# A new order of the last cross attention, and the last head pair's sums of exponentials from TensorE alone

## The reference, cut to what matters

```python
x = layernorm(x + L1_attn(x))       # L1_attn returns x + softmax(q k^T / 8) v w_o
x = layernorm(x + L1_xattn(ctx, x)) # the change ends here
x = layernorm(x + L1_ffn(x))        # 4 experts, two chosen for each token

def L1_xattn(x, latents, mask, ...):       # x: 154 context rows, latents: 512 rows
    xn, ln = layernorm(x, ...), layernorm(latents, ...)
    q  = ln @ Wq.T
    kv = concat([xn @ Wkv.T, ln @ Wlkv.T], axis=1)      # 154 + 512 keys
    k, v = kv[..., :128], kv[..., 128:]                 # 2 heads of 64
    qn, kn = rmsnorm(q, qn_g) * 64 ** -0.5, rmsnorm(k, kn_g)
    attn = softmax(where(mask, qn kn^T, -max))
    return (attn @ v) @ Wo.T + bo
```

## Time and profile before

| | us |
|---|---|
| median of 3 runs | 696.09 (694.47 to 698.51) |
| profiled execution | 697.45 |
| its span, first to last instruction | 695.7 |

### The profile page before, as it was taken

One profiled execution on the slowest core, in us unless ns is written; L12 is line 12 of the kernel. 1 busy time (PEld: TensorE's weight loads), 2 busy tenths in 40 slices (PEclk: granted clock), 3 DMA queues, 4 the chain that ended last, 5 costly groups with the idle time before them and its releaser, 6 DMA issues.

```text
span 695.7 us, 8771 instructions
## 1 busy us (share of the span) xinstructions
PE 617.9 (89%) x3161; PEld 307.6 (44%) x3162; DVE 451.1 (65%) x1172; ACT 287.3 (41%) x548; POOL 246.7 (35%) x178
## 2 busy tenths in 40 slices
PE   8766769998997899999999979997878999999996
PEld 4322457976752322222224422333522446565655
DVE  6999998457679457666765597687626673333234
ACT  7979966032403564444443344341141342212120
POOL 2897443233501554554464444572150100000001
PEclk9957979999998999999999999998997999999999
DMA  8200032030000000000000000001400000000000
GB/s 316 93 0 0 2 121 124 1 122 1 1 1 0 0 1 0 1 0 1 2 0 1 1 0 1 0 1 63 195 0 1 1 1 1 0 1 0 1 1 31
DMA packets 3681, 18.92 MB, mean 27 GB/s; under 512 B 917, under 2 KB 2198, under 8 KB 3126
## 3 DMA queue, kind: packets, MB, share of 16 engines
q1 hardware_dynamic: 3638, 18.36, 6.9%
HBM read 17.84 MB, written 0.52 MB: 26 GB/s over the span
## 4 chain that ended last, share of the span: by engine, by line
PE 62%; DVE 20%; ACT 9%; issue 5%; POOL 4%; POOLq 0%; DVEq 0%; ACTq 0%
PE PS L2339 10%; PE PS L1617 8%; PE PS L2353 6%; DVE SB L1846 6%; PE PS L1562 4%; PE PS L1601 4%; PE PS L1585 3%; PE PS L1687 2%; PE PS L1631 2%; PE PS L2063 2%; DVE SB L199 2%; PE PS L2074 1%; DVE SB L1868 1%; ACT SB L468 1%; POOL SB L238 1%
## 5 line engine op out<-in xcount | busy, mean ns | idle before, releaser
L1832 POOL TENSOR_TENSOR SB<-SB 128x1024 f32<-128x1024 f32 x32 | 75.3, 2353 | 115.3 <-ACT SB L1785 115.3
L1846 DVE TENSOR_REDUCE SB<-PS 128x2 f32<-128x1024 f32 x64 | 78.4, 1225 | 56.7 <-PE PS L1585 56.7
L1785 ACT ACTIVATE SB<-PS 128x1024 f32<-128x1024 f32 x64 | 65.5, 1023 | 101.3 <-PE PS L1604 101.2
L2339 PE MATMUL PS<-SB 128*128 128x512 f32 x176 | 83.1, 609 | 0.2 <-DVE SB L2416 0.2
L1617 PE MATMUL PS<-SB 128*64 128x512 f32 x256 | 69.9, 628 | 1.4 <-DVE SB L1871 1.4
L1601 PE MATMUL PS<-SB 64*128 64x512 f32 x256 | 68.9, 616 | 1.1 <-ACT SB L1789 1.1
L238 POOL TENSOR_TENSOR SB<-SB 128x4 f32<-128x4 f32 x18 | 19.4, 1078 | 133.0 <-DVE SB L204 132.9
L2391 ACT ACTIVATE SB<-PS 128x512 f32<-128x512 f32 (+1 forms) x48 | 28.5, 596 | 90.2 <-PE PS L2339 87.3
L2416 DVE TENSOR_TENSOR SB<-SB,PS 128x512 f32<-128x512 f32 (+1 forms) x48 | 32.6, 686 | 48.1 <-PE PS L2339 43.7
L2353 PEld LDWEIGHTS PS<-SB 128*128 128x128 f32 (+1 forms) x384 | 49.4, 190 | 18.5 <-issue 10.0
L1868 DVE RECIPROCAL SB<-PS 128x512 f32<-128x512 f32 x16 | 53.7, 3355 | 3.9 <-PE PS L1631 3.9
(11 more groups left out here) (401 smaller groups left out, 1132.8 us busy)
## 6 DMA issues: line engine op xcount, KB each, us to landing
SB<-exp SPq DMA_DIRECT2D x1, 4352.0 KB, 14.0
SB<-moe SPq DMA_DIRECT2D x1, 4096.0 KB, 12.3
SB<-dft SPq DMA_DIRECT2D x1, 2304.0 KB, 12.1
SB<-att SPq DMA_DIRECT2D x1, 2048.0 KB, 8.1
SB<-mix SPq DMA_DIRECT2D x1, 768.5 KB, 4.5
SB<-mix SPq DMA_DIRECT2D x1, 640.0 KB, 5.6
SB<-ssm SPq DMA_DIRECT2D x1, 602.0 KB, 6.7
SB<-lat SPq DMA_DIRECT2D x1, 585.0 KB
```

The costliest lines, as they stand in the source:

```text
L1785: act.activation(expd[i % 2][:, 1024 * u:1024 * u + 1024], bank(2 * (u % 2), 2), ACT.Exp).then_inc(sem("d_exp"), 1)
L1832: pool.tensor_tensor(half_sums[half], e[:, 0:1024], e[:, 1024:], ALU.add).then_inc(sem("d_half_sum"), 1)
L1846: dve.tensor_reduce(shift[i % 2][:, qt:qt + DK + 1:DK], two_heads(bank(4, 2)), AX_X, ALU.max, negate=True)\
L2339: pe.matmul(bank(2 * (i % 3) + side), exp_w["e_w13"][:, c:c + 128], xsT[:, 512 * n:512 * n + 512], start=True, stop=True).then_inc(sem(("t ...
```

## The change

It does the following.
- Pair 16's sums: GpSimd's three adds for it go; `sums(15)` multiplies the ones by the four chunks of exponentials, eight matmuls. Its `weigh` writes bank 0 instead of 6 and no longer waits for pair 15's product; the output projection goes to bank 6 instead of 0.
- The two turns of batch 0's rows move behind the context's, out of the loop; the four `weigh` and the sums of pair 16 stand together ahead of all `e_maxima(0, ...)`, which are spread over the output projection, the last one behind it.
- GpSimd makes the powers k = 0 to 2 at the same place as before.
- VectorE takes maximum(0, 0), then pair 16's reciprocal and product, maxima 1 and 2, the residual add and its statistics, maximum 3, and `shift_in(0)` behind the second norm's statistics.
- Cross attention, batch 0: the turn of the normalized rows stands ahead of `score(0, 0)`, the projections of batch 1's rows behind it, their turns behind `score(0, 3)` and `weigh(0, 2)`, batch 1's maxima among the last scores and weighs, `shifts(1)` ahead of `sums(0)`. ScalarE and VectorE follow; VectorE's `late_sum` stands between batch 1's maxima 1 and 2.

```diff
@@ -1564,6 +1564,9 @@
+    def heads_bank(i):
+        return bank(6 if i < NP_ - 1 else 0)
+
@@ -1610,25 +1613,32 @@
-                if i >= 1:
+                if 1 <= i < NP_ - 1:
...
-                ins = pe.matmul(bank(6)[head(h), :], v, expd[i % 2][:, 1024 * kt + 512 * h:1024 * kt + 512 * h + 512],
+                ins = pe.matmul(heads_bank(i)[head(h), :], v, expd[i % 2][:, 1024 * kt + 512 * h:1024 * kt + 512 * h + 512],
...
         def sums(i):
-            pe.wait_ge(sem("d_key_sum"), i + 1)
+            if i < NP_ - 1:
+                pe.wait_ge(sem("d_key_sum"), i + 1)
+                parts = [key_sum]
+            else:
+                pe.wait_ge(sem("d_exp"), 4 * NP_)
+                parts = [expd[i % 2][:, 1024 * kt:1024 * kt + 1024] for kt in range(4)]
...
-            for h in range(2):
-                ins = pe.matmul(bank(7)[DK * h:DK * h + DK, :], ones[:, 0:DK], two_heads(key_sum)[:, h, :], start=True, stop=True)
+            for k, part in enumerate(parts):
+                for h in range(2):
+                    ins = pe.matmul(bank(7)[DK * h:DK * h + DK, :], ones[:, 0:DK], two_heads(part)[:, h, :],
+                                    start=(k == 0), stop=(k == len(parts) - 1))
@@ -1676,7 +1686,7 @@
-                    pe.matmul(bank(0)[:, 128 * t:128 * t + 128], headed[:, at:at + 128],
+                    pe.matmul(bank(6)[:, 128 * t:128 * t + 128], headed[:, at:at + 128],
@@ -1733,9 +1743,6 @@
-                if i == NP_ - 1 and u == 3:
-                    e_turn_tiles(pe, 0)
-                    e_turn_tiles(pe, 1)
@@ -1745,23 +1752,25 @@
-        weigh(last, 0)
-        weigh(last, 1)
+        e_turn_tiles(pe, 0)
+        e_turn_tiles(pe, 1)
+        for kt in range(4):
+            weigh(last, kt)
+        sums(last)
         e_maxima(pe, 0, 0)
-        weigh(last, 2)
-        weigh(last, 3)
+        pe.wait_ge(sem("d_headed"), last)
+        pe.matmul(bank(6), zeros_low, mask_16[0:1, 0:512], start=True, stop=False)
+        attended_part((0,))
         e_maxima(pe, 0, 1)
-        sums(last)
-        pe.matmul(bank(0), zeros_low, mask_16[0:1, 0:512], start=True, stop=False)
-        attended_part((0, 1))
+        attended_part((1, 2))
         e_maxima(pe, 0, 2)
-        attended_part((2, 3))
-        e_maxima(pe, 0, 3)
+        attended_part((3,))
...
-            ins = pe.matmul(bank(0)[:, 128 * t:128 * t + 128], headed[:, 512 * last + 128 * t:512 * last + 128 * t + 128],
+            ins = pe.matmul(bank(6)[:, 128 * t:128 * t + 128], headed[:, 512 * last + 128 * t:512 * last + 128 * t + 128],
...
+        e_maxima(pe, 0, 3)
@@ -1820,10 +1829,7 @@
     def d_pool(pool):
-        for i in range(NP_):
-            if i == NP_ - 1:
-                for k in range(3):
-                    e_pool_row_norms(pool, k)
+        for i in range(NP_ - 1):
@@ -1835,6 +1841,8 @@
+        for k in range(3):
+            e_pool_row_norms(pool, k)
@@ -1868,7 +1876,7 @@
-            dve.tensor_tensor(headed[:, 512 * i:512 * i + 512], bank(6), unit, ALU.mult).then_inc(sem("d_headed"), 1)
+            dve.tensor_tensor(headed[:, 512 * i:512 * i + 512], heads_bank(i), unit, ALU.mult).then_inc(sem("d_headed"), 1)
@@ -2018,7 +2026,7 @@
     def rough_at(b, qt):
-        return 512 * (1 if b == 0 else 0 if qt % 2 else 5)
+        return 512 * (1 if b == 0 else 0 if qt == 2 else 5)
@@ -2030,10 +2038,10 @@
-        if n == 5:
+        if n == 6:
             pe.wait_ge(sem("d_exp"), 4 * NP_ + KT)
-        if b == 0 and qt or b == 1 and qt >= 2:
-            pe.wait_ge(sem("d_max"), 4 * NP_ + n - b)
+        elif qt:
+            pe.wait_ge(sem("d_max"), 4 * NP_ + n - n // 7)
@@ -2049,14 +2057,12 @@
         def shifts(b):
             pe.wait_ge(sem("d_max"), 4 * NP_ + 4 * b + 4)
-            pe.transpose(bank(6)[:, 0:128], e_shift[b], ident).then_inc(sem("d_shifts"), 1)
+            pe.transpose(bank((7, 6)[b])[:, 0:128], e_shift[b], ident).then_inc(sem("d_shifts"), 1)
         def score(b, u):
...
-            if n == 0:
-                pe.wait_ge(sem("e_attended"), 3)
@@ -2078,7 +2084,7 @@
         def sums(b):
             if b == 0:
-                pe.wait_ge(sem("d_max"), 4 * NP_ + 7)
+                pe.wait_ge(sem("d_max"), 4 * NP_ + 8)
@@ -2101,25 +2107,31 @@
+        turn_half(pe, tiled(xn), "e_normed", 1, 1, 5)
         score(0, 0)
-        for u in range(KT):
-            if u + 1 < KT:
-                score(0, u + 1)
-            if u == 2:
-                turn_half(pe, tiled(xn), "e_normed", 1, 1, 5)
-            weigh(0, u)
-            if u == 3:
-                e_project(pe, 4)
-                e_project(pe, 5)
-            if u == 4:
-                e_project(pe, 6)
-                e_project(pe, 7)
+        e_project(pe, 4)
+        e_project(pe, 5)
+        score(0, 1)
+        e_project(pe, 6)
+        e_project(pe, 7)
+        weigh(0, 0)
+        score(0, 2)
+        weigh(0, 1)
+        score(0, 3)
         e_turn_tiles(pe, 2)
+        weigh(0, 2)
         e_turn_tiles(pe, 3)
-        for qt in range(4):
-            e_maxima(pe, 1, qt)
+        score(0, 4)
+        weigh(0, 3)
+        e_maxima(pe, 1, 0)
+        score(0, 5)
+        e_maxima(pe, 1, 1)
+        weigh(0, 4)
+        weigh(0, 5)
+        e_maxima(pe, 1, 2)
+        e_maxima(pe, 1, 3)
+        shifts(1)
         sums(0)
-        shifts(1)
@@ -2147,26 +2159,25 @@
         def turned_rows(b):
-            act.wait_ge(sem("e_qk_turned"), 2 * b + 1)
+            act.wait_ge(sem("e_qk_turned"), b + 2)
...
+        act.wait_ge(sem("e_qk_turned"), 1)
+        act.activation(k3[:, :, 0:256], c4, ACT.Copy, scale=lat["kn_g"]).then_inc(sem("e_qk_T"), 1)
         turned_rows(0)
-        act.wait_ge(sem("e_qk_turned"), 2)
-        act.activation(k3[:, :, 0:256], c4, ACT.Copy, scale=lat["kn_g"]).then_inc(sem("e_qk_T"), 1)
+        e_normed_in(act, 1)
...
+                if b == 0 and u < 2:
+                    e_rows_in(act, 2 * u + 4)
+                    e_rows_in(act, 2 * u + 5)
                 if b == 0 and u == 3:
-                    e_normed_in(act, 1)
-                if b == 0 and u >= 4:
-                    e_rows_in(act, 2 * u - 4)
-                    e_rows_in(act, 2 * u - 3)
-            if b == 0:
-                turned_rows(1)
+                    turned_rows(1)
@@ -2212,9 +2223,9 @@
         def low(b):
-            dve.wait_ge(sem("e_qk_T"), 3 * b + 1)
+            dve.wait_ge(sem("e_qk_T"), 2 * b + 2)
             dve.tensor_copy(q_16[b], q_T[b]).then_inc(sem("e_qk_16"), 1)
-            dve.wait_ge(sem("e_qk_T"), 3 * b + 2)
+            dve.wait_ge(sem("e_qk_T"), 2 * b + 3)
@@ -2228,7 +2239,7 @@
         def shift_in(b):
...
-                              bank(6)[:, None, 0:128].to_broadcast([P, 4, 128]),
+                              bank((7, 6)[b])[:, None, 0:128].to_broadcast([P, 4, 128]),
@@ -2239,35 +2250,37 @@
-        low(0)
-        dve.wait_ge(sem("e_qk_T"), 3)
+        dve.wait_ge(sem("e_qk_T"), 1)
...
+        low(0)
...
+        headed_of(NP_ - 1)
         maximum(0, 1)
-        headed_of(NP_ - 1)
         maximum(0, 2)
-        maximum(0, 3)
...
-        dve.scalar_tensor_tensor(xsum[:, c], xs[:, c], 2.0, bank(0), ALU.mult, ALU.add).then_inc(sem("e_attended"), 1)
+        dve.scalar_tensor_tensor(xsum[:, c], xs[:, c], 2.0, bank(6), ALU.mult, ALU.add).then_inc(sem("e_attended"), 1)
...
-        shift_in(0)
+        maximum(0, 3)
...
+        shift_in(0)
...
-        dve.wait_ge(sem("d_exp"), 4 * NP_ + 5)
-        dve.tensor_tensor(late_sum, weights[0][:, 3072:4096], weights[0][:, 4096:5120], ALU.add).then_inc(sem("e_second_sum"), 1)
...
-        for qt in range(4):
-            maximum(1, qt)
+        maximum(1, 0)
+        maximum(1, 1)
+        dve.wait_ge(sem("d_exp"), 4 * NP_ + 5)
+        dve.tensor_tensor(late_sum, weights[0][:, 3072:4096], weights[0][:, 4096:5120], ALU.add).then_inc(sem("e_second_sum"), 1)
+        maximum(1, 2)
+        maximum(1, 3)
```

## The result

The changed kernel takes 699.91 us (median of 20 runs, 696.64 to 704.76) against 697.94 us before (20 runs, 694.06 to 701.77). The ratio of the means is 1.0034 with a 95% interval of 1.0018 to 1.0049: 2.4 us slower (2.0 by the medians). 699.1 was forecast, from a median of 696.09.

What follows compares the result with a forecast made beforehand. Bound by a chain of handovers between engines, no engine full. Up to the norm's last apply -3.65 us, from there +6.6, together +3.0: 699.1 us from the median 696.09; range 695.0 to 703.0.

Steps and rivals of the forecast that it cites:

- d_out ends: End of pair 16's output projection on TensorE: forecast at 490.9 us, against 494.2 before.
- e_normed: VectorE's last apply of the norm, which every score now waits for: forecast at 499.4 us, 3.65 us earlier.
- powers start: GpSimd's powers k=3 and 4 for batch 1's rows, behind two adds and the bias add: forecast at 515.5 us.
- wait ahead of the turn: TensorE's new wait ahead of the first turn of batch 1's rows, until GpSimd's power and the scaling: 6.5 us.
- Rival C: Faster: GpSimd's order does not bind, the first turn of batch 1's rows need not wait; 690.9 us, chance 0.08.
- rival A: The forecast: GpSimd's queue holds back the turn of batch 1's rows by 6.5 us; 699.1 us, chance 0.55.
- The front: Pair 16 and its output, up to the norm's last apply: forecast to gain 3.65 us.
- The tail: From the norm's last apply to batch 1's first score: forecast to lose 6.6 us.
- I count no drop: TensorE's 2.4 us wait ahead of sums(0): clock assumed not to fall; if it falls, +1.7 us.
- rival B: Slower: same waits, but low clock lasts longer or falls again before sums(0); 701 to 704 us, chance 0.27.
- The power's price: GpSimd's power k=3, the one unsure term: 1.77 us by spacing taken, printed span 2.55; the latter adds 0.8.
- Moving shifts ahead of sums(0) costs the same: Batch 1's start: shift_in leaves the path but sums(0) waits for the last maximum, so both orders cost the same.

Runs made afterwards that it cites:

- e1: Changed kernel with GpSimd making power k=3 ahead of its first add of exponentials and k=4 ahead of the second; ratio to before 1.0010.
- e2: Changed kernel with both powers k=3 and 4 ahead of GpSimd's adds, which wait until VectorE has scaled the rows; ratio to before 0.9976.
- e8: As e2, but GpSimd's adds wait until VectorE has also cast batch 1's rows, and the bias add waits for late_sum; ratio to before 0.9911.
- e7: Changed kernel with matmuls of ones on a free bank in TensorE's four waits; ratio to before 0.9959.
- e6: Kernel before with only the change's first part, up to d_out; everything behind it and GpSimd's order as before; ratio to before 0.9969.
- e9: e8 with matmuls of ones in TensorE's three remaining waits; 689.76 us, ratio to before 0.9875.
- e3: Changed kernel with only GpSimd's bias add moved behind the powers k=3 and 4; ratio to before 1.0045.
- e5: Changed kernel with pair 16's sums as before: GpSimd's three adds back, then four passes instead of 16; ratio to before 1.0050.
- e4: Changed kernel with score(0,0) and its exponential ahead of the normalized rows' turn, and shift_in(0) ahead of the second norm's statistics; ratio to before 1.0080.
- e10: e4 with matmuls of ones in TensorE's waits; ratio to before 0.9970.

## Why the prediction was right, point by point

In the prediction's own times, with the changed kernel's rows moved back by the 1.82 us of its later entry:

| step | forecast | measured |
|---|---|---|
| d_out ends | 490.9 | 489.3 |
| e_normed | 499.4 | 497.8 |
| exp(0,2) ends | 510.5 | 508.9 |
| powers start | 515.5 | 513.55 |
| wait ahead of the turn | 6.5 | 6.05 |
| first turn starts | 518.2 | 516.1 |
| score(1,0) | 536.8 | 536.4 |
| sum against before | +3.0 | +2.6 |

- The mechanism held: the powers started behind the bias add, the turn waited for them, and e1, e2 and e8 removed that wait by GpSimd's order alone. Rival C (the order does not bind) is excluded by the trace, rival A was the case. That the sum came out within 0.4 us is in part luck: two terms were off by more, in opposite directions.
- The front was sized 1.6 us too dear. I took 1.01 us for four passes of weighs and sums, a distance that ran from a weigh to a score. Sixteen passes of one kind in a row take 3.48 us (472.88 to 476.36), 0.2175 a pass instead of 0.2525, and the two groups of sixteen save 1.1 us; the turns gave 0.3 more (0.97 us for four tiles, not 1.2).
- The tail was sized 1.2 us too cheap (38.6 us from e_normed to score(1,0), 37.4 forecast): 0.5 too dear up to the first turn, 1.7 too cheap behind it. The term that failed most is "I count no drop" at the 2.4 us wait ahead of sums(0): the clock fell (0.50 over 534 to 536) and the 12 passes took 4.11 us instead of 3.05. The clock's part in this is 1.4, since at full speed the 12 passes take 2.80 (e2, e7). For the same reason 3.05 was no price for the 4.62 us before: the low clock held for 3.7 us of them, not 2.7. The low clock behind the 6 us wait also lasted longer, 5.3 us (back at 523.3) instead of 3.5. Both errors are rival B's: its condition, that the clock falls again before sums(0), came true, at a smaller price than its 701 to 704, and the front's surplus paid for it.
- The power's price: two powers in 3.25 us, and 1.68 from the start of the first to the scaling. The price that I chose was right. But nothing here shows the 2.55 us of k=3 in the kernel before to be a faulty span. It stands in just two traces, before and e6, and in both VectorE's `late_sum`, with two SBUF inputs, starts 0.17 us ahead of the power; everywhere else in this stretch one such power shows 1.64 to 1.75 us, and two in a row show 3.25 to 3.27. This is the row of before that belongs to k=3 in the earlier trace rows:
```profile
513.34 1.22 DVE L2264 TENSOR_TENSOR SB<-SB 128x1024 f32<-128x1024 f32 x1
```
  So the power was most likely held up by VectorE, as VectorE is elsewhere by GpSimd; no run moves `late_sum` alone. The Trainium skill (Perfetto Trace Analysis, GPSIMD Engine Instruction) asks for start-to-start spacing instead of spans; in this case's rows the two agree, with 1.73 us from the power to the add behind it in e1 and a span of 1.75.
- "Moving shifts ahead of sums(0) costs the same" was not tested: no run has the other order behind the same wait. What the clock cost there in the new order is said above.
- Filling TensorE's waits gained 5.45 us (e7). Taking queue and lock away gained 8.7 (e8), both together 11.6 (e9): they overlap by 2.6, since a wait that goes takes its low clock along. The sums are of one trace each; by the ratios of the runs the overlap is 2.7. The order of the change without them is 9.0 us faster than the kernel before, but the fair comparison is the 6.2 of e8, since no run fills the waits of the kernel before. The change's idea was sound and was undone by a list on one engine that it did not touch.

Not settled: why the entry into the stretch varies between 463.8 and 469.0 us from run to run (it lies in code that no kernel here changes). Part of it is the clock: ahead of 460 us the mean granted clock was 0.95 in the three traces that enter first (e2, e8 and before, by 465.4) and 0.94 in the nine others.

## What to carry to other kernels

When work is moved later on one engine, go through the in-order lists of all the others for what stands behind the instructions that wait for it; here tiny powers (1.7 us) stood behind three adds, two of which wait for exponentials. When an engine's instruction is freed, look at what it will now meet: in e1, e2 and e3 a gain of 1 to 4 us went into the next lock. A wait of TensorE can cost twice, once by itself and once by the low clock behind it, and where the wait cannot go, idle matmuls on a free bank take the second part away.

## What the runs showed of the hardware

- GpSimd's adds of 128x1024 hold up some of VectorE's instructions and leave others alone. A float32 scaling with two SBUF inputs took 5.05 us (e5) and 5.06 us (e1) for 0.76, casts from SBUF to bf16 2.22 and 2.57 us for 0.43 (e2). Maxima read from PSUM kept their 1.55 us (e8), a reciprocal its 3.35 (e5), and so did a sum over SBUF rows; these are VectorE's rows beside the changed kernel's first add, 507.14 to 509.49:
```profile
508.34 0.69 DVE L2194 TENSOR_REDUCE SB<-SB 128x8 f32<-128x512 f32 x1 [1.87 <-ACT SB L2150]
509.06 0.46 DVE L2195 TENSOR_SCALAR SB<-SB 128x8 f32<-128x8 f32 x1
```
  The sum took the same 0.69 us as elsewhere, the small TENSOR_SCALAR 0.46 for 0.17, and 1.38 in e1. The Trainium skill (SBUF — State Buffer, Who interferes with whom) describes an exclusive lock between the two engines, which casts and instructions with two SBUF inputs can meet; for casts it says that whoever issues first has it for the whole instruction. These rows agree. What I had not expected is that the loser can lose twice in a row: 5.06 us is two GpSimd instructions, since each of the two scalings met one (the longest single one took 2.57 us).
- A wait of TensorE of 2.4 us can go either way from one kernel to the next. Ahead of shifts(1) it stands in seven kernels. In six of them (changed, e1, e3, e4, e5, e8) the clock was at 0.50 within the 12 passes behind it, which took 4.17 to 4.49 us. In e2 it stayed at full speed, though it had been low shortly before (0.52 over 520 to 522):
```profile
527.02 0.33 PE L2061 MATMUL PS<-SB 128*128 128x128 f32 x1 [2.40 <-DVE SB L2237]
527.28 2.80 PE L2099 MATMUL PS<-SB 128*64 128x512 f32 x12
```
- The way back to full speed varies too. Behind the wait for e_normed the same instructions ran at 1.2 GHz for 3.1 us in the changed kernel and e8, 4.7 us in e5 and 5.2 us in e2. In e4, where gaps of about 1 us stood between the first of them, it was 11.6 us. That the gaps are the reason is not shown, since e10 filled them and the waits ahead of them together.
